# A selective scan's order on three engines, its first chunk's preparation moved among the last projections, and one product moved from GpSimd to ScalarE

## The chip, the cores and the metric
The kernel runs on one core of one Trainium2 chip. Its engines are TensorE (PE in the profile; PEld is its loading of weights), VectorE (DVE), ScalarE (ACT), GpSimd (POOL) and SyncE (SP), which here only issues transfers. The metric is the device time of one execution in microseconds (us), from the runs given below; lower is better.

## The reference, cut to what matters
The input x is (8, 256, 32, 32): 8 batches, 256 channels, N = 1024 tokens. There are 2 heads of 128 channels, 8 states, and a fixed permutation of the tokens for each head.
```
xn  = layernorm(x, over channels)
x_ssm, res, gate = split(silu(in_proj_w (768x256) @ xn + in_proj_b))
xf  = silu(depthwise conv of 3 taps along the tokens (x_ssm))
dbc = dbc_w (34x256) @ xf + dbc_b     # for each head: 1 dt, 8 B, 8 C
dt  = softplus(dbc[:, :, 0])
x_h, dt, B, C = tokens in the order perm[head]
# scan, for each batch and head:
h   = exp(dt_t * A) * h + dt_t * B_t * x_t ;  y_t = C_t . h  + D * x_t
y   = y in the tokens' own order * silu(gate) + res
x   = x + silu(out_proj_w @ y + out_proj_b)
t   = layernorm(x, over channels, by tokens)
x   = t + sum over 8 experts of soft gate[e] * (t @ expert_w[e] + expert_b[e])
```
The last line is added to the tokens before that layernorm. Softmax weights of the gate under 0.1 are dropped and the rest scaled to a sum of 1.

## The kernel before
The whole program is written out by hand for each engine: every engine has a queue of instructions in the written order, and semaphores tie them together. `Signal` wraps a semaphore that is counted up a fixed number of times per batch or chunk. `x_ready.at(q, k)` is the value after k steps of unit q.

**Projections, 0 to about 250 us.** Eight batches, one after the other, some 28.7 us each. PE does in_proj in three products of split fp32 values for six row blocks (`in_proj(b, par, m0, m1)`, m = 0 to 5; m = 0 and 1 are x_ssm, 2 and 3 res, 4 and 5 gate); each m is two groups of six matmuls, L1064. ACT applies silu (`silu_of`, `silu_xf`, `gate_silu`). DVE does layernorm statistics, the convolution (`convolve(b, m)`) and, for each batch, a part of the ranks of the permutation (`ranks`, then `places`, which turns them into addresses). PE's `dbc_by_tokens` (L1074) gives dt, B and C. POOL computes softplus in two parts (`softplus_front`, L592 to L600, and `softplus_back`, L607 to L630) and rstd (`deviations`, L564). POOL also scatters the tokens' numbers to their places in the order, in 16 indirect transfers (`scatter_order(h)`, L644; 8 for head 0 at the end of batch 5, 8 for head 1 at the end of batch 6). SP stores the rows of a batch (x, dt, B, C by tokens: `store_rows`, L442), res (L482) and gate (L490), and loads the order once into `turn` (L463).

**The scan, about 261 to 509 us.** 16 chunks: two groups of four batches, eight chunks of 128 tokens each, which are two blocks of 64 (SUB = 64). A chunk holds ST = 8 tiles, one for each head and batch. For chunk q:

- POOL gathers its rows in the head's order (`gather_rows`, L669, two indirect transfers), three chunks ahead.
- PE `sums_of(q)` (L1102, L1103) sums dt within the blocks. DVE `flatten` (L1631) rearranges B and C, `exponents` (L1638 to `cs`, L1644 to `args`) multiplies the sums by A.
- PE `rows_of` (L1113, L1115) turns B and C to rows. ACT `rows_high` (L850, L854, L856) and DVE `rows_low` (L1662, L1664) split them into high and low parts. ACT `block_decays` (L863). SP `spread` stores these rows (L449) and loads them spread out (L454 into `cr`, named `xhl` or `cr` in the trace, and L456 into `bl`).
- `up_to_token`: dt times a triangle of ones, into `dtri` (L679, POOL). PE `times_of` (L1122, L1124) sums it, DVE `distances` (L1652) subtracts.
- For each state s = 0 to 7: ACT `decays` (L921, exp), PE `products` (L1185, B by C, into three banks in turn), DVE `times_decay` (L1701, their product), POOL `add_state` (L708, sum over states 0 to 6 into `ksum`, `sm` in the trace), then DVE `whole_kernel` (L1713, two instructions: ksum plus state 7 into `kbd`).
- The state carried between blocks: DVE `weigh` (L1677, L1681), PE `states` (L1135) and `columns` (L1142), ACT `columns` (L868 into `cwt`), DVE `next_states` (L1689, L1695), ACT `states_by_tile` (L937, eight scaled copies of 128 columns).
- PE `y_of(q, i)` (L1194: states by C; L1197: x by kbd) for head i, ACT `y_rows` (L927), SP `store_y` (L498). y_of(q-1) runs among the products of chunk q, and so do y_rows(q-1) and whole_kernel(q-1).

The body of chunk q on each engine, before:
```
PE:   rows_of(q+1), products 0-2, times_of(q+1), product 3, y_of(q-1,0), products 4-5,
      y_of(q-1,1), sums_of(q+2), products 6-7, states(q+1), columns(q+1)
ACT:  decays 0-1, rows_high(q+1), block_decays(q+1), decays 2-3, y_rows(q-1,0), decays 4-5,
      y_rows(q-1,1), states_by_tile(q), decays 6-7, columns(q+1)
DVE:  times_decay 0, whole_kernel(q-1), rows_low(q+1), distances(q+1), times_decay 1-3,
      weigh(q+1), times_decay 4-5, flatten(q+2), times_decay 6, exponents(q+2), times_decay 7, next_states(q+1)
POOL: add_state 0-6, up_to_token(q+2), gather_rows(q+3)
SP:   spread(q+1), store_y(q-1)
```
The first chunk is prepared behind the last batch's projections: POOL gathers chunks 0 and 1 once `turn` has landed; PE does sums_of(0) after in_proj m = 4. The last three chunks' places on POOL's queue hold the first gathers of y (`gather_first`, L718).

**The rest, to the end.** For each of 16 half batches: gather y back to the tokens' order, gate, out_proj, layernorm and the experts (L1322), where PE is busy nearly all of the time.

Of the kernel before, what the change touches and what calls it, by code (L numbers as in the profile page):

```python
# [61 lines left out]
def metaformer(nc, x, in_w, in_b, dw_w, dw_b, dbc_w, dbc_b, a_log, d_par, mobius, out_w, out_b,  # L62
# [26 lines left out]
    with ExitStack() as ctx:  # L89
# [126 lines left out]
        ksum = sm[:, 0:4, :].rearrange("p s n -> p (s n)")  # L216
# [3 lines left out]
        names = ysb[1][:, 0:2, :].rearrange("p a n -> p (a n)").bitcast(U32).rearrange("p (j w) -> p j w", w=16)  # L220
# [180 lines left out]
        def _(sync):  # L401
# [142 lines left out]
        def _(pool):  # L544
# [94 lines left out]
            def scatter_order(h):  # L639

                pool.wait_ge(place_ready, 1)
                part_waits(pool)
                for t in range(NT):
# [40 lines left out]
            softplus_front(NB - 2)  # L684
# [6 lines left out]
            up_to_token(Chunk(0))  # L691
            softplus_back(NB - 2)
# [5 lines left out]
            def add_state(c, s):  # L698

                pool.wait_ge(bc_used[s % 3].sem, bc_used[s % 3].at(c.q, s // 3 + 1))  # L700
                if s == 0:
                    pool.wait_ge(dskip_ready, 2)
                    pool.wait_ge(k_ready.sem, k_ready.at(c.q, 0))
                else:
                    pool.wait_ge(summed.sem, summed.at(c.q, s))
                tiles = (v.rearrange("p (t n) -> p t n", n=SUB) for v in (ksum, ee[:, s, :]))
# [17 lines left out]
            def body(q):  # L724
# [3 lines left out]
                if q + 2 < CHUNKS:  # L728
                    up_to_token(Chunk(q + 2))
# [58 lines left out]
        def _(act):  # L788
# [80 lines left out]

            def batch(b):  # L870
# [14 lines left out]
                silu_xf(b, 1)  # L885
                act.wait_ge(gate_stored.sem, gate_stored.at(b, 0))
# [36 lines left out]

            def y_rows(c, h):
# [15 lines left out]
            def body(q):  # L940
# [5 lines left out]
                decays(c, 2, 4)  # L946
                if q:
                    y_rows(Chunk(q - 1), 0)
                else:
                    stage_rows(NB - 1, 0, 1)  # L950
                decays(c, 4, 6)
                if q:
                    y_rows(Chunk(q - 1), 1)
                else:
                    stage_rows(NB - 1, 1, 4)
                states_by_tile(c)
                decays(c, 6, S)
# [51 lines left out]
        def _(pe):  # L1009
# [134 lines left out]
            def batch(b):  # L1144
# [4 lines left out]
                in_proj(b, par, 1, 5)  # L1149
                if ahead:  # L1150
                    normalised_x(b + 1)
# [230 lines left out]
        def _(dve):  # L1382
# [197 lines left out]
            def places():  # L1580

                own.did(dve.tensor_reduce(idxb[:, :, :], racc[:, :, :, :], AX.X, ALU.add))
                own.settle()
                for h in range(HEADS):
                    own.did(dve.tensor_scalar(placef[:, h, :], idxb[:, h, :], float(h * N), None, ALU.add))
                own.settle()
                own.did(dve.tensor_copy(place[:, :, :], placef[:, :, :]))
                own.did(dve.tensor_copy(names, bc(token[:, :, :].rearrange("p t h -> p (t h)"), 2, 16)))
                own.settle()
                dve.sem_inc(place_ready, 1)  # L1590

# [9 lines left out]

            RANKS = {1: (0, 4), 2: (4, 8), 3: (8, 12), 4: (12, 16)}

            def batch(b):
                par, ahead = b % 2, b + 1 < NB
                own1 = Steps(dve, dve1, b + 1)
                if b:
                    dbc_in(b - 1)
                convolve(b, 0)
                if ahead:  # L1610
                    statistics(own1, b + 1)
                convolve(b, 1)
# [8 lines left out]
                if b in RANKS:  # L1621
                    ranks(*RANKS[b])
                if b == 4:
                    places()
# [79 lines left out]
            def whole_kernel(c):  # L1704
# [6 lines left out]
                for i in range(2):  # L1711
                    rr = slice(SUB * i, SUB * i + SUB)
                    dve.tensor_tensor(kbd[rr, :, rr], ksum[rr, :].rearrange("p (s n) -> p s n", s=ST),  # L1713
# [3 lines left out]
            def body(q):  # L1717
                c = Chunk(q)
                times_decay(c, 0)
                if q:  # L1720
                    whole_kernel(Chunk(q - 1))
# [3 lines left out]
                for s in range(1, 4):  # L1725
                    times_decay(c, s)
# [23 lines left out]
            for k in range(2):  # L1750
                dve.wait_ge(mm_full[k].sem, mm_full[k].at(NB - 1, 0))
            dve.memset(cr[0].bitcast(F32), 0.0).then_inc(cr_zero, 1)
            first, second = Chunk(0), Chunk(1)
            flatten(first)
            exponents(first)
# [9 lines left out]
            for i in range(2):  # L1765
                dve.wait_ge(mm_full[i].sem, mm_full[i].at(NB, 0))
            dve.memset(cr[1].bitcast(F32), 0.0).then_inc(cr_zero, 1)
            own.did(dve.memset(batch_no[:, :], 0.0))
            dve.tensor_copy(idxf[:, :, :], idxb[:, :, :]).then_inc(place_ready, 1)
            dve.wait_ge(place_ready, 2)  # L1770
# [215 lines left out]
```

## Time and profile before
| | us |
|---|---|
| median of 3 runs | 1070.61 (1068.48 to 1070.85) |
| the profiled execution, its own time | 1064.97 |
| its span, first to last instruction | 1063.2 |
| PE busy | 930.4 (88%) |
| DVE busy | 771.3 (73%) |
| ACT busy | 508.6 (48%) |
| POOL busy | 505.9 (48%) |
| mean granted clock of TensorE | 0.917 |

Durations come from the one profiled execution, which took a little less than the median of the runs. Busy shares are over the whole span; the stage that the change touches is about a quarter of it. The granted clock is a share of TensorE's full 2.4 GHz; 0.50 is 1.2 GHz. In a timeline a line with xN stands for N instructions in a row, and the bracket gives the engine's idle time before it and what ended it. One name of a tile may be another's: the tiles xin, xtm and xr hold the gathered rows in turn, ysb or ssm or rg what their stage keeps there.

### The profile page before, as it was taken

To read this page: it belongs to the slowest core of one execution; us is meant where nothing else is said; L and a number is where in the kernel's file an instruction comes from. 1 tells how busy PE (TensorE), PEld (TensorE's weight loads), DVE (VectorE), ACT (ScalarE), POOL (GpSimd) and SP (SyncE) were. 2 spreads that over 40 slices of the span, in tenths; PEclk is the share of its full clock that TensorE was granted. 3 is DMA by queue.
4 is the path that set the end of the run, shared out by engine and by line. 5 is a ranking of instruction groups with operands and counts; after the bars stand their busy time and mean duration, and the time that the engine had idled before them with its cause. 6 is when DMAs were issued, how large, how long until landed. Compare 5 with 4: busy or idle time off the path is not lost.

```text
span 1063.2 us, 15454 instructions
## 1 busy us (share of the span) xinstructions
PE 930.4 (88%) x4658; PEld 718.6 (68%) x4658; DVE 771.3 (73%) x2001; ACT 508.6 (48%) x924; POOL 505.9 (48%) x563
## 2 busy tenths in 40 slices
PE   4999999986687678666499999999999999999997
PEld 3887888874454445444367777777777777877776
DVE  5768887534677778775458787787787877878775
ACT  2777877664666665666223333332333323333330
POOL 2066666775887877788650333313333132330000
PEclk8999999996777887778689999999999999999999
DMA  5335674476254343334331131401314013140001
GB/s 162 119 89 171 190 191 147 116 175 177 76 144 126 98 120 109 117 108 156 126 133 44 33 145 39 147 30 39 138 39 158 21 38 138 39 158 20 20 1 39
DMA packets 63687, 110.05 MB, mean 104 GB/s; under 512 B 18538, under 2 KB 44436, under 8 KB 60564
## 3 DMA queue, kind: packets, MB, share of 16 engines
q1 hardware_dynamic: 56468, 91.41, 27.4%
q0 software_dynamic: 7168, 18.03, 5.9%
q8 instruction: 22, 0.36, 0.1%
q14 instruction: 29, 0.24, 0.1%
HBM read 61.51 MB, written 47.92 MB: 103 GB/s over the span
## 4 chain that ended last, share of the span: by engine, by line
PE 69%; DVE 7%; ACT 7%; issue 5%; POOL 5%; DMA 4%; ACTq 0%; SPq 0%; DVEq 0%; another core or an unknown queue 0%; POOLq 0%
PE bank L1322 31%; PE bank L1064 8%; PE bank L1230 4%; PE bank L1255 4%; PE bank L1185 3%; ACT xf L937 3%; PE bank L1283 2%; PE bank L1074 2%; PE bank L1194 2%; POOL sm L708 2%; PE bank L1197 2%; PE bank L1122 2%; PE bank L1092 2%; DMA score_scratch<-score 1%; PE bank L1267 1%
## 5 line engine op out<-in xcount | busy, mean ns | idle before, releaser
L763 POOL TENSOR_TENSOR ssm<-ssm,rg 128x512 f32<-128x512 f32 x30 | 35.2, 1192 | 269.7 <-DVE ssm L1799 269.7
L751 POOL DMA_INDIRECT xtm<-y_scratch,idxu x120 | 119.2, 993 | 68.6 <-issue 34.2
L1322 PE MATMUL bank<-wexph,xhl 128*128 128x512 f32 x512 | 144.9, 405 | 0.1
L1322 PE MATMUL bank<-wexph,cr 128*128 128x512 f32 x512 | 143.4, 401 | 0.1
L708 POOL TENSOR_TENSOR sm<-sm,rg 128x512 f32<-128x512 f32 x96 | 122.4, 1275 | 30.0 <-DVE rg L1701 20.1
L1701 DVE TENSOR_TENSOR rg<-rg,bank 128x512 f32<-128x512 f32 x128 | 83.2, 681 | 60.6 <-ACT rg L921 39.9
L1322 PEld LDWEIGHTS bank<-wexph,xhl 128*128 128x128 f32 x512 | 93.8, 189 | 23.4 <-DVE xf L1903 2.0
L1322 PEld LDWEIGHTS bank<-wexph,cr 128*128 128x128 f32 x512 | 93.4, 189 | 22.0 <-DVE ysb L1903 1.7
L921 ACT ACTIVATE rg<-dists,aown 128x512 f32<-128x512 f32 x128 | 84.7, 714 | 0.0
L1322 PE MATMUL bank<-wexpl,xhl 128*128 128x512 f32 x256 | 80.6, 396 | 0.0
L1322 PE MATMUL bank<-wexpl,cr 128*128 128x512 f32 x256 | 80.3, 395 | 0.0
L1898 DVE SCALAR_TENSOR_TENSOR ysb<-bank,soft,ysb 128x256 f32<-128x256 f32 x128 | 58.3, 479 | 25.1 <-PE bank L1322 23.0
L1898 DVE SCALAR_TENSOR_TENSOR xf<-bank,soft,xf 128x256 f32<-128x256 f32 x128 | 57.8, 479 | 24.4 <-PE bank L1322 21.5
L1064 PE MATMUL bank<-xhl,winh 128*128 128x512 f32 x192 | 55.0, 408 | 4.0 <-ACT ssm L813 2.0
L1064 PE MATMUL bank<-cr,winh 128*128 128x512 f32 x192 | 55.5, 412 | 3.1 <-ACT ssm L813 2.8
L1322 PEld LDWEIGHTS bank<-wexpl,xhl 128*128 128x128 f32 x256 | 48.3, 189 | 11.6
L1322 PEld LDWEIGHTS bank<-wexpl,cr 128*128 128x128 f32 x256 | 48.1, 188 | 11.3
L1903 DVE SCALAR_TENSOR_TENSOR xf<-bank,soft,xf 128x256 f32<-128x256 f32 x128 | 55.5, 475 | 0.0
L1903 DVE SCALAR_TENSOR_TENSOR ysb<-bank,soft,ysb 128x256 f32<-128x256 f32 x128 | 55.5, 475 | 0.0
L813 ACT ACTIVATE rg<-bank,inb 128x512 f32<-128x512 f32 x64 | 43.5, 686 | 14.6 <-PE bank L1064 13.6
L927 ACT ACTIVATE ysb<-bank 128x512 f32<-128x512 f32 x32 | 19.1, 598 | 64.0 <-PE bank L1197 63.6
L592 POOL TENSOR_TENSOR sp<-euler,sp 128x16 f32<-128x16 f32 x8 | 24.4, 3056 | 48.0 <-DVE sp L1563 47.9
(303 smaller groups left out, 2111.9 us busy)
## 6 DMA issues: line engine op xcount, KB each, us to landing
xin<-in_x SPq DMA_DIRECT2D x16, 1024.0 KB, 5.3
res_gate_scratch<-rg SPq DMA_DIRECT2D x16, 1024.0 KB, 10.9
rg<-res_gate_scratch SPq DMA_DIRECT2D x8, 2048.0 KB
y_scratch<-ysb SPq DMA_DIRECT2D x16, 512.0 KB, 3.6
out<-stage SPq DMA_DIRECT2D x16, 512.0 KB, 2.7
rows_scratch<-xr SPq DMA_DIRECT2D x8, 580.0 KB
rows_scratch<-stage SPq DMA_DIRECT2D x8, 580.0 KB
bc_scratch<-r SPq DMA_DIRECT2D x16, 288.0 KB
```

The lines of the kernel that those rows point to most:

```text
L708: pool.tensor_tensor(total, bc(dskip[:, :], 1, ST) if s == 0 else total, new, ALU.add).then_inc(summed.sem, 1)
L751: pool.indirect_dma_start(out=xtm[:, t, h * P:(h + 1) * P], out_offset=None, in_=y_d[b // GB].rearrange("q p s c -> (q p s) c"), in_offset ...
L763: pool.tensor_tensor(z[:, k, :], z[:, k, :], rg[:, k, cols], ALU.add).then_inc(z_ready.sem, 1)
L813: act.activation(dst, bank[2 + hf][:, :], ACT.Silu, bias=inb[:, m:m + 1]).then_inc(mm_used[hf].sem, 1)
L921: act.activation(ee[:, s, :], dist[c.two].rearrange("p t n -> p (t n)"), ACT.Exp, scale=aown[:, s:s + 1]).then_inc(e_ready.sem, 1)
L1064: last = pe.matmul(bank[2 + hf][:, :], w[:, k, m * P:(m + 1) * P], v[:, k, cols], start=(n + k == 0), stop=(n + k == 3))
L1230: last = pe.transpose(dst[:, i * P:(i + 1) * P], src(i), ident[:, :])
L1255: last = pe.matmul(bank[2 + m][:, :], w[:, k, m * P:(m + 1) * P], x_[:, k, :], start=(n + k == 0), stop=(n + k == 3))
L1322: last = pe.matmul(bank[4 + i][:, :], x_[:, k, i * P:(i + 1) * P], w[:, 2 * ep * KC + k:2 * ep * KC + k + KC + 1:KC, :], start=(n + k == 0 ...
L1701: dve.tensor_tensor(ee[:, s, :], ee[:, s, :], bank[BC_BANK + s % 3][:, :], ALU.mult).then_inc(bc_used[s % 3].sem, 1)
L1898: dve.scalar_tensor_tensor(ttm[par][:, i, :], bank[4 + i][:, 0:C], soft[par][:, 2, i, 2 * ep:2 * ep + 1], ttm[par][:, i, :], ALU.mult, ALU ...
L1903: dve.scalar_tensor_tensor(ttm[par][:, i, :], bank[4 + i][:, C:2 * C], soft[par][:, 2, i, 2 * ep + 1:2 * ep + 2], ttm[par][:, i, :], ALU.m ...
```

## The change
Seven things, the first four ahead of the scan:

1. `scatter_order` takes a quarter at a time: head 0 at the ends of batches 3 and 4, the first half of head 1 at the end of batch 5, its second half in batch 6 between deviations(7) and softplus_back(5). `places(h)` is computed at batches 2 and 4 for one head each.
2. On POOL, softplus_front(6) moves behind the gathers of chunks 0 and 1 and up_to_token(0).
3. store_rows(6) moves from SP's queue to ACT's, behind silu_of(7, 5).
4. The first chunk is prepared between the last projections: on PE sums_of(0) after m = 2, rows_of(0) and times_of(0) after m = 3, and dbc_by_tokens(7) after m = 4. On DVE the zeroing of cr[0] moves to the start of batch 7, and flatten(0) and exponents(0) between its two convolutions. On ACT rows_high(0) and block_decays(0) move ahead of silu_of(7, 4).
5. `ksum` is doubled, so add_state(q, 0) waits for whole_kernel(q-2) rather than whole_kernel(q-1).
6. up_to_token(q+2) is ACT's: eight ACTIVATE Copy of 64 columns with dt as the scale by partition.
7. The chunk's order, by the diff's bodies: ACT issues decays 2 to 7, states_by_tile(q), both y_rows(q-1), up_to_token(q+2), columns(q+1). PE issues products 0 and 1, rows_of(q+1), product 2, times_of(q+1), product 3, the rest as before. On DVE whole_kernel(q-1) moves behind times_decay 1, and exponents(q+2) ahead of times_decay 6.

The diff, cut to its core:
```diff
-        ksum = sm[:, 0:4, :].rearrange("p s n -> p (s n)")
+        ksum = [sm[:, 4 * i:4 * i + 4, :].rearrange("p s n -> p (s n)") for i in range(2)]
...
-                    store_rows(b - 1)
                     sync.wait_ge(cr_zero, 1)
...
-                for t in range(NT):
+            def scatter_order(h, part):
+                for t in range(part * TPH, (part + 1) * TPH):
...
                 deviations(b + 1)
+                if b == NB - 2:
+                    scatter_order(1, 1)
                 if b:
                     softplus_back(b - 1)
...
-                if b == NB - 3:
-                    scatter_order(0)
-                if b == NB - 2:
-                    scatter_order(1)
+                if NB - 5 <= b < NB - 2:
+                    scatter_order(*divmod(b - NB + 5, 2))
...
-            softplus_front(NB - 2)
             pool.wait_ge(order_loaded, 16 * HEADS)
...
             up_to_token(Chunk(0))
+            softplus_front(NB - 2)
             softplus_back(NB - 2)
...
-                    pool.wait_ge(k_ready.sem, k_ready.at(c.q, 0))
+                    if c.q:
+                        pool.wait_ge(k_ready.sem, k_ready.at(c.q - 1, 0))
...
-                if q + 2 < CHUNKS:
-                    up_to_token(Chunk(q + 2))
                 if q == 0:
                     softplus_back(NB - 1)
...
+                if not ahead:
+                    act.wait_ge(consts_ready, 1)
+                    rows_high(Chunk(0))
+                    block_decays(Chunk(0))
                 act.wait_ge(gate_stored.sem, gate_stored.at(b, 0))
                 silu_of(b, 4)
...
+                silu_of(b, 5)
                 if not ahead:
-                    act.wait_ge(consts_ready, 1)
-                    rows_high(Chunk(0))
-                    block_decays(Chunk(0))
-                silu_of(b, 5)
+                    store_rows(b - 1)
...
+            def up_to_token(c):
+
+                act.wait_ge(xr_ready[c.row].sem, xr_ready[c.row].at(c.turn4, 32))
+                act.wait_ge(b_full.sem, b_full.at(c.q, 0))
+                for t in range(ST):
+                    last = act.activation(dtri[:, t, :], tri[:, :], ACT.Copy, scale=dt_of(c)[:, t:t + 1])
+                last.then_inc(dtri_ready.sem, 1)
...
-                decays(c, 2, 4)
                 if q:
-                    y_rows(Chunk(q - 1), 0)
+                    decays(c, 2, S)
+                    states_by_tile(c)
+                    for h in range(HEADS):
+                        y_rows(Chunk(q - 1), h)
...
+                if q + 2 < CHUNKS:
+                    up_to_token(Chunk(q + 2))
                 if q + 1 < CHUNKS:
                     columns(Chunk(q + 1))
...
+                    in_proj(b, par, 1, 3)
                     pe.wait_ge(consts_ready, 1)
                     pe.wait_ge(rows_staged.sem, rows_staged.at(b - 1, 4))
                     sums_of(Chunk(0))
-                    dbc_by_tokens(b)
+                    in_proj(b, par, 3, 4)
                     rows_of(Chunk(0))
                     times_of(Chunk(0))
+                    in_proj(b, par, 4, 5)
+                    dbc_by_tokens(b)
                     in_proj(b, par, 5, MI)
...
+                products(c, 0, 2)
                 if q + 1 < CHUNKS:
                     rows_of(Chunk(q + 1))
-                products(c, 0, 3)
+                products(c, 2, 3)
...
+                if not ahead:
+                    zero_rows(0, NB - 1)
                 convolve(b, 0)
                 if ahead:
                     statistics(own1, b + 1)
+                else:
+                    flatten(Chunk(0))
+                    exponents(Chunk(0))
                 convolve(b, 1)
...
                 times_decay(c, 0)
-                if q:
-                    whole_kernel(Chunk(q - 1))
                 if q + 1 < CHUNKS:
                     rows_low(Chunk(q + 1))
                     distances(Chunk(q + 1))
-                for s in range(1, 4):
-                    times_decay(c, s)
+                times_decay(c, 1)
+                if q:
+                    whole_kernel(Chunk(q - 1))
+                times_decay(c, 2)
+                times_decay(c, 3)
...
                 if q + 2 < CHUNKS:
                     flatten(Chunk(q + 2))
+                    exponents(Chunk(q + 2))
                 times_decay(c, 6)
-                if q + 2 < CHUNKS:
-                    exponents(Chunk(q + 2))
                 times_decay(c, 7)
```

## Rows read from the trace of the kernel before
**Rows 1.** Windows: us; busy us (count) PE, PEld, DVE, ACT, POOL; PEclk, DMA share, GB/s.
```profile
325.10:355.80 30.70, 22.48 (x114) 14.95 (x113) 23.84 (x48) 19.52 (x51) 24.04 (x21) 0.78 0.38 112
...
426.30:429.40 3.10, 0.00 (x0) 0.00 (x0) 1.01 (x4) 2.82 (x8) 2.62 (x3) 1.00 0.36 93
...
430.20:437.00 6.80, 6.23 (x14) 3.82 (x14) 6.14 (x14) 3.83 (x11) 4.89 (x6) 0.50 0.45 128
...
214.00:226.00 12.00, 9.24 (x62) 8.01 (x62) 0.78 (x5) 5.78 (x9) 9.85 (x9) 0.97 1.08 269
```

**Rows 2.** Chain of waits, 428 to 448 us: start, us, what.
```profile
441.07 2.43 ACT xf L937 x8
```

**Rows 3.** Timeline, chunk 430 to 444 us: start, us, engine, line, operation, idle before.
```profile
430.69 1.32 ACT L921 ACTIVATE rg<-dists,aown 128x512 f32<-128x512 f32 x2
...
432.85 0.28 ACT L856 ACTIVATE r<-bank 64x128 fp32r<-64x128 f32 x1
...
433.21 1.44 DVE L1713 TENSOR_TENSOR kbd<-sm,rg 64x512 f32<-64x512 f32 x2
...
434.69 0.48 DVE L1662 TENSOR_TENSOR r<-bank,r 64x64 fp32r<-64x64 f32 x3
...
436.13 1.87 DVE L1701 TENSOR_TENSOR rg<-rg,bank 128x512 f32<-128x512 f32 x3
...
436.89 6.95 POOL L708 TENSOR_TENSOR sm<-sm,rg 128x512 f32<-128x512 f32 x5 [0.79 <-DVE rg L1701]
...
438.57 1.02 PE L1194 MATMUL bank<-xf,cwt 128*128 128x512 f32 x2
...
439.43 1.05 PE L1197 MATMUL bank<-xr,kbd 128*128 128x128 f32 x8
...
440.58 0.60 ACT L927 ACTIVATE ysb<-bank 128x512 f32<-128x512 f32 x1 [0.40 <-PE bank L1197]
```

**Rows 4.** Timeline at the scan's end, POOL and DVE.
```profile
512.45 2.76 POOL L773 TENSOR_TENSOR ssm<-ssm,stage 128x512 f32<-128x512 f32 x2 [3.74 <-DVE ssm L1943]
513.01 2.75 DVE L1713 TENSOR_TENSOR kbd<-sm,rg 64x512 f32<-64x512 f32 x2
```

**Rows 5.** Timeline of PE, chunks 14 and 15.
```profile
478.55 1.63 PE L1185 MATMUL bank<-xhl,bl 128*128 128x512 f32 x3
...
491.59 2.44 PE L1185 MATMUL bank<-cr,bl 128*128 128x512 f32 x4 [3.01 <-DMA bl<-bc_scratch]
...
494.60 2.04 PE L1194 MATMUL bank<-xf,cwt 128*128 128x512 f32 x2 [0.57 <-issue]
...
496.43 1.91 PE L1197 MATMUL bank<-xr,kbd 128*128 128x128 f32 x8
```

**Rows 6.** Timelines of POOL and SP's queue, ahead of the scan.
```profile
212.87 2.15 SPq L442 DMA_DIRECT2D rows_scratch<-stage  x2
...
222.14 0.96 POOL L644 DMA_INDIRECT order_scratch<-ysb,place  x1 [0.30 <-issue]
...
227.71 1.42 SPq L463 DMA_DIRECT2D turn<-order_scratch  x2
...
232.00 1.62 POOL L669 DMA_INDIRECT xin<-rows_scratch,turn  x1 [1.97 <-DMA turn<-order_scratch]
...
246.01 1.08 SPq L449 DMA_DIRECT2D bc_scratch<-r  x1
...
254.19 2.73 SPq L454 DMA_DIRECT2D xhl<-bc_scratch  x8
...
262.45 1.26 POOL L708 TENSOR_TENSOR sm<-dskip,rg 128x512 f32<-128x512 f32 x1 [4.70 <-DVE rg L1701]
```

**Rows 7.** Timeline of PE, last batch to first chunk.
```profile
231.94 1.21 PE L1064 MATMUL bank<-cr,winh 128*128 128x512 f32 x4
...
238.24 0.36 PE L1102 MATMUL bank<-xin,cumu 128*128 128x8 f32 x2 [0.46 <-issue]
...
260.74 1.65 PE L1185 MATMUL bank<-xhl,bl 128*128 128x512 f32 x3 [9.56 <-DMA bl<-bc_scratch]
```

More of the change, by code:

```diff
@@ L219, in metaformer @@
               for i in (1, 2) for j in range(8)]
-        names = ysb[1][:, 0:2, :].rearrange("p a n -> p (a n)").bitcast(U32).rearrange("p (j w) -> p j w", w=16)
+        names = ysb[0][:, 0:2, :].rearrange("p a n -> p (a n)").bitcast(U32).rearrange("p (j w) -> p j w", w=16)
         z = ssm[:, :, 0:HALF]
@@ L637, in low_experts @@
                                    ALU.subtract).then_inc(wexp_low, 1)
[L639 to L641 removed]
+            def scatter_order(h, part):
+                pool.wait_ge(place_ready, h + 1)
                 part_waits(pool)
[L643 removed]
+                for t in range(part * TPH, (part + 1) * TPH):
                     pool.indirect_dma_start(
@@ L702, in add_state @@
                     pool.wait_ge(dskip_ready, 2)
-                    pool.wait_ge(k_ready.sem, k_ready.at(c.q, 0))
+                    if c.q:
+                        pool.wait_ge(k_ready.sem, k_ready.at(c.q - 1, 0))
                 else:
                     pool.wait_ge(summed.sem, summed.at(c.q, s))
-                tiles = (v.rearrange("p (t n) -> p t n", n=SUB) for v in (ksum, ee[:, s, :]))
+                tiles = (v.rearrange("p (t n) -> p t n", n=SUB) for v in (ksum[c.two], ee[:, s, :]))
                 total, new = tiles
@@ L868, in columns, with store_rows @@
                 act.activation(cwt[c.four][:, :], bank[A_BANK][:, 0:P], ACT.Copy).then_inc(a_free.sem, 1)
+            def store_rows(b):
+                act.wait_ge(rows_ready.sem, rows_ready.at(b, 4))
+                act.wait_ge(rows_staged.sem, rows_staged.at(b, 4))
+                for hf, v in enumerate(staged[b % 2]):
+                    act.dma_start(rows_d[b // GB][:, hf * TPH * HEADS:(hf + 1) * TPH * HEADS, b % GB, :],
+                                  v.rearrange("p t (h c) -> p (t h) c", h=HEADS)).then_inc(rows_stored[b % 2].sem, 16)
             def batch(b):
@@ L945, in body @@
                     block_decays(Chunk(q + 1))
-                decays(c, 2, 4)
                 if q:
-                    y_rows(Chunk(q - 1), 0)
+                    decays(c, 2, S)
+                    states_by_tile(c)
+                    for h in range(HEADS):
+                        y_rows(Chunk(q - 1), h)
                 else:
+                    decays(c, 2, 4)
                     stage_rows(NB - 1, 0, 1)
-                decays(c, 4, 6)
-                if q:
-                    y_rows(Chunk(q - 1), 1)
-                else:
+                    decays(c, 4, S)
                     stage_rows(NB - 1, 1, 4)
-                states_by_tile(c)
-                decays(c, 6, S)
+                    states_by_tile(c)
+                if q + 2 < CHUNKS:
+                    up_to_token(Chunk(q + 2))
                 if q + 1 < CHUNKS:
@@ L1148, in batch @@
                     x_by_tokens(b + 1)
-                in_proj(b, par, 1, 5)
                 if ahead:
+                    in_proj(b, par, 1, 5)
                     normalised_x(b + 1)
@@ L1578, in ranks, with places, rows_by_rank @@
                     own.settle()
-            def places():
-                own.did(dve.tensor_reduce(idxb[:, :, :], racc[:, :, :, :], AX.X, ALU.add))
+            def places(h):
+                own.did(dve.tensor_reduce(idxb[:, h, :], racc[:, h, :, :], AX.X, ALU.add))
                 own.settle()
-                for h in range(HEADS):
-                    own.did(dve.tensor_scalar(placef[:, h, :], idxb[:, h, :], float(h * N), None, ALU.add))
+                own.did(dve.tensor_scalar(placef[:, h, :], idxb[:, h, :], float(h * N), None, ALU.add))
                 own.settle()
-                own.did(dve.tensor_copy(place[:, :, :], placef[:, :, :]))
-                own.did(dve.tensor_copy(names, bc(token[:, :, :].rearrange("p t h -> p (t h)"), 2, 16)))
+                own.did(dve.tensor_copy(place[:, h, :], placef[:, h, :]))
+                if h == 0:
+                    own.did(dve.tensor_copy(names, bc(token[:, :, :].rearrange("p t h -> p (t h)"), 2, 16)))
                 own.settle()
                 dve.sem_inc(place_ready, 1)
+            def rows_by_rank():
                 own.did(dve.tensor_copy(idxu[:, :, :], idxb[:, :, :]))
@@ L1600, in places, with zero_rows @@
                 ts(idxb[:, 1, :], idxb[:, 1, :], float(SUB * ST), None, ALU.add)
+            def zero_rows(i, b):
+                for hf in range(2):
+                    dve.wait_ge(mm_full[hf].sem, mm_full[hf].at(b, 0))
+                dve.memset(cr[i].bitcast(F32), 0.0).then_inc(cr_zero, 1)
             RANKS = {1: (0, 4), 2: (4, 8), 3: (8, 12), 4: (12, 16)}
@@ L1622, in batch @@
                     ranks(*RANKS[b])
+                if b in (2, 4):
+                    places(b // 2 - 1)
                 if b == 4:
-                    places()
+                    rows_by_rank()
             def flatten(c):
@@ L1712, in whole_kernel @@
                     rr = slice(SUB * i, SUB * i + SUB)
-                    dve.tensor_tensor(kbd[rr, :, rr], ksum[rr, :].rearrange("p (s n) -> p s n", s=ST),
+                    dve.tensor_tensor(kbd[rr, :, rr], ksum[c.two][rr, :].rearrange("p (s n) -> p s n", s=ST),
                                       ee[rr, S - 1, :].rearrange("p (s n) -> p s n", s=ST),
@@ L1749, in _ @@
                 batch(b)
-            for k in range(2):
-                dve.wait_ge(mm_full[k].sem, mm_full[k].at(NB - 1, 0))
-            dve.memset(cr[0].bitcast(F32), 0.0).then_inc(cr_zero, 1)
             first, second = Chunk(0), Chunk(1)
-            flatten(first)
-            exponents(first)
             rows_low(first)
@@ L1764, in _ @@
             next_states(first)
-            for i in range(2):
-                dve.wait_ge(mm_full[i].sem, mm_full[i].at(NB, 0))
-            dve.memset(cr[1].bitcast(F32), 0.0).then_inc(cr_zero, 1)
+            zero_rows(1, NB)
             own.did(dve.memset(batch_no[:, :], 0.0))
             dve.tensor_copy(idxf[:, :, :], idxb[:, :, :]).then_inc(place_ready, 1)
-            dve.wait_ge(place_ready, 2)
+            dve.wait_ge(place_ready, 3)
             dve.tensor_copy(idxu[:, :, :], idxf[:, :, :]).then_inc(idx3_ready.sem, 1)
```

1 line of the change is left out of this document (removed).

## The prediction
> **What bounds the kernel now.** I read the page first, then windows, then the chain. The page's busy shares name PE, but the change touches only the scan and its preparation, so what counts is what ends last there. Two scan chunks take 30.70 us, 15.35 each, in which PE is busy 22.48, DVE 23.84, POOL 24.04 and ACT 19.52 [rows 1]: no engine is full, so the chunk is a ring of waits. The chain of waits runs on PE through products, times_of and both y_of, then on ACT through the copy of y and states_by_tile (2.43 us [rows 2]), which hold back decay 6 and with it exponents and states. Second, PE's clock: it idles 3.10 us before states, and the 6.80 us that begin 0.8 us later are granted 0.50, 1.2 GHz, not 2.4 [rows 1]. Those slow microseconds now fall on rows_of, products 0 to 3, times_of and the head of the first y_of. The reader is to see that the low clock is paid by whatever follows PE's idle time. Third, the front: chunk 0's first product waits for a row of steps that begins with the load of the order and the first gather; that is worked out below.
>
> **The steady chunk, part by part.** Below, "first y_of" is y_of(q-1, 0).
>
> *Order.* ACT now issues decays 2 to 7 and states_by_tile ahead of both y copies, so decay 6 no longer waits behind y_of and the 2.43 us of states_by_tile; that stall goes. What is late next is y_of itself: whole_kernel, which PE's y_of waits for, moves from behind times_decay 0 to behind rows_low, distances and times_decay 1. PE has nothing between product 3 and y_of. Behind the waiting y_of are products 4 and 5, and behind those times_decay 4 and 5 on DVE, add_state on POOL, and exponents(q+2).
>
> *dt times the triangle.* POOL's one instruction becomes eight ACT copies with a pointer scale, 64 columns each. The nearest row has eight of 128 columns in 2.43 us [rows 2]. Bounds: 1.2 us, by the halved columns alone, and 2.43. I take 1.9, as a copy of the same form is unlikely to lose more than a quarter with half its columns. It stands on ACT between the last y copy and columns(q+1), whose copy is what rows_of(q+2) and the next pair of decays wait for.
>
> *The ring of the new order, at full clock.* Two decays, then rows_high, from 430.69 to the end of its last copy 433.13: 2.4 [rows 3]. rows_low and distances, 434.69 to the start of the next at 436.13: 1.4. times_decay 1, one of three in 1.87 us: 0.6. whole_kernel 1.4. First y_of, from 438.57 to 439.43 + 1.05: 1.9 [rows 3]. Products 4 and 5: 0.5 (three take 1.63 at half clock [rows 5]). Second y_of 1.9. ACT's y copy 0.6 [rows 3], dtri copies 1.9, columns copy 0.3 (as the one at 432.85 [rows 3]), waits between engines some 0.3. Sum 13.3; of the first term about 0.5 is ACT's wait for PE and the previous state, and about 0.2 laps over: 12.6.
>
> *The port of DVE and POOL.* In the scan whole_kernel now takes 1.44 for two, as POOL only issues gathers then. Where POOL ran two adds beside it, it took 2.75 [rows 4]. Both changes bring adds there: whole_kernel comes later, and add_state(q, 0) needs only k_ready of chunk q-2, as ksum is doubled. Bounds 0 and 1.3; I take 1.1, since POOL's adds are close together (five in 6.95 [rows 3]) and can start right after times_decay 0. Ring: 13.7. The Trainium skill ("SBUF — State Buffer", Who interferes with whom) says that a DVE instruction with two SBUF inputs and a GpSimd one exclude each other on a shared port pair for their whole length; it speaks against this move, and the trace agrees [rows 4]. By that rule the ring is 13.7, and without it 12.6.
>
> *The clock.* PE's idle time now lies between product 3 and y_of: distances' tail, times_decay 1 and whole_kernel, 0.7 + 0.6 + 1.4 + 1.1, which is 3.8, or 2.7 without the port wait. That is about as long as the 3.10 us that a half-clock stretch follows today, and y_of would then be what stands in it: at half clock it took 3.7 us in chunk 15 (494.60 to 496.43 + 1.91), against 1.9 [rows 3, 5]. If the low stretch covers the first y_of and products (+1.8, +0.5) and half of what is left (+1.1) it costs 3.4; if it falls on times_of and the products, which lie beside DVE's work, 0. I take 2.0. Ring: 15.7 against 15.35, +0.35 a chunk; over the 12 intervals from chunk 2 to 14: **+4.2**.
>
> **The front.** Scatter quarters (0,0) to (1,0) move to batches 3 to 5, where POOL waits for DVE's statistics anyway; without that cover each is 5.1 us. Quarter (1,1) now stands before softplus_back(5): four of 1.26 [rows 6] delay it by 5.1 us, so SP's store_rows(5), at 212.87 now [rows 6], goes at 217.9, and behind it on SP the res and gate stores and then the turn load L463. The load's own wait ends earlier (its last scatter, at 222.14 now, is done by 212), but it is issued at about 222, right behind stores that now take the 12 us from 214 to 226 at a share of 1.08 (269 GB/s, 3.2 MB [rows 1]) and that start some 5 us later. It lands at 231 to 233, and the first gather, at 232.00 now [rows 6], comes no earlier. softplus_front(6), behind up_to_token(0) now, took nothing off this path.
> PE now reaches sums_of(0) after m=2, at 231.9, where m=3 stood [rows 7]; sums_of waits until about 239 (238.24 now). m=3 and m=4, 5.8 us together (231.94 to 238.24 less the gap of 0.46), come after it. rows_of stands behind m=3, which may find the clock fallen: 2.9 us, or 5.8 at half. So rows_of starts at 242 to 245 and, with some 3 us of ACT's copies and rows_low (an estimate), the rows leave for bc_scratch at about 248. They are no longer behind store_rows(6), so I put their landing at 3 to 4 us, not the 8.2 from the issue at 246.01 to L454 at 254.19 [rows 6]; from L454 to the product is 6.55 [rows 6, 7]. First product: 258 to 260, against 260.74. The memset before convolve(7,0) lies beside PE's wait; without that cover it delays the last convolution by its length.
> store_rows(6), on ACT behind silu_of(7,5) and so behind in_proj m=5, leaves when m=5 is done, some 258; gather(2), for which it is waited, precedes POOL's first add: 266 to 268 (262.45 now [rows 6]). The seven adds then run unbroken (five in 6.95 [rows 3]: 9.8) and no dtri follows, so POOL catches up. Chunk 2 begins 1 us earlier: **-1** (bounds -3 and +3).
>
> **The tail.** From chunk 14 to 15 it is 13.04 now [rows 5]; there the new ring has no dtri copies: 13.8, **+0.7**.
>
> Sum: -1 + 4.2 + 0.7 = +3.9 on the profiled execution's 1064.97 us, 1068.9. The runs' median, 1070.61, is 1.0053 times that execution: 1074.5.
>
> **Rivals.** 0.2% (2.1 us) is about what a measurement of this kernel can tell from no change.
> A, the other side: *the clock stays up through y_of*. For it: y_of is longer than states was, and the idle time may come out under 3.1 us; if the port wait is absent too, it is 1.1 shorter. Against: the row of 3.10. The period is 13.7, or 14.2 with a remainder of low clock: 12 x (-1.65 or -1.15), with front and tail, is -20 or -14, a run of 1050 or 1056; without the port wait too it would be less still. It decides from a period under 15.2. Chance 0.22.
> B, faster too: *the turn load is not held by the stores*, and lands at 227: sums_of comes 5 us earlier, PE hardly waits, and chunk 2 starts 7 us earlier. -7 + 4.2 + 0.7 = -2.1 to -4: 1067.5. The full DMA engines of those 12 us [rows 1] speak against it. Chance 0.15.
> C: *the change does nothing that shows*: DVE's 23.84 us a pair plus the port wait make the period 15.3, whatever the order; front and tail cancel. 1068.5 to 1072.7. Chance 0.21.
> Forecast, +2.2 to +12: 0.42; its own range 1073 to 1083.
> Faster 0.37, same 0.21, slower 0.42. Range: up to 1083, where the low clock costs 2.7 a chunk; down to 1055, which leaves out the fuller part of A.
>
> **What would show it.** Two chunks against 30.70. L1713: 1.44 for two now [rows 3], 2.5 if the port is shared. L1194 and L1197: their half-clock lengths on the first y_of, and where PE's idle window stands. The eight copies: 1.9 us together. Dates of the first gather, sums_of(0), first product, first add. If y_of runs at its 1.9 in most chunks, A is true and my sign is wrong; if L463 lands by 228, B.

## The result and the profile after

The changed kernel takes 1076.12 us (median of 20 runs, 1069.23 to 1083.51), the kernel before 1067.20 (20 runs, 1063.58 to 1070.85) in the same sessions. The ratio is 1.0079, with a 95% interval of 1.006 to 1.0097: 8.4 us slower (the medians alone would give 8.9). The forecast was slower by 0.36%. The profiled execution of the changed kernel is also its fastest, 1069.23 us, 4.3 us over that of the kernel before, so the traces show only about half of the difference.

The windows of the two chunks from 356.10 to 386.80, to be held against [rows 1]; the columns are us, busy us (count) of PE, PEld, DVE, ACT and POOL, then PEclk, DMA share and GB/s:

```profile
356.10:386.80 30.70, 20.93 (x113) 13.82 (x112) 28.43 (x48) 23.16 (x67) 22.16 (x19) 0.89 0.38 113
```

DVE is busy for 28.43 of 30.70 us, where it was 23.84. Nothing was added to its work. PE's mean clock even rose, from 0.78 to 0.89. DVE, nearly full, is now the engine that bounds a chunk.

From the first times_decay of chunk 2 to that of chunk 14 the changed kernel needs 187.90 us, 15.66 a chunk; before it was 184.23, 15.35. The two rows in the timeline of DVE, then the same two of the kernel before:

```profile
292.92 0.69 DVE L1737 TENSOR_TENSOR rg<-rg,bank 128x512 f32<-128x512 f32 x1
...
480.82 0.69 DVE L1737 TENSOR_TENSOR rg<-rg,bank 128x512 f32<-128x512 f32 x1
```

```profile
295.21 0.69 DVE L1701 TENSOR_TENSOR rg<-rg,bank 128x512 f32<-128x512 f32 x1 [1.68 <-PE bank L1185]
...
479.44 0.69 DVE L1701 TENSOR_TENSOR rg<-rg,bank 128x512 f32<-128x512 f32 x1 [0.90 <-PE bank L1185]
```

The mean hides a difference. In this fastest execution chunks 4 to 9 take 15.35 us each on average, exactly as before. Of the 3.67 us that the twelve chunks lose, 2.2 lie in chunks 2 and 3 and 1.1 in chunks 11 to 13.

One chunk of the changed kernel in its timeline (start, us, engine, line, operation, idle before), to be held against [rows 3]. L1749 is whole_kernel, L708 the add, L1214 and L1217 are y_of, L1713 is weigh, L1667 flatten, L937 the eight copies of dt times the triangle:

```profile
404.87 0.67 DVE L1737 TENSOR_TENSOR rg<-rg,bank 128x512 f32<-128x512 f32 x1
404.98 1.28 POOL L708 TENSOR_TENSOR sm<-dskip,rg 128x512 f32<-128x512 f32 x1
405.46 3.03 DVE L1749 TENSOR_TENSOR kbd<-sm,rg 64x512 f32<-64x512 f32 x2
406.40 1.54 POOL L708 TENSOR_TENSOR sm<-sm,rg 128x512 f32<-128x512 f32 x1
...
408.59 1.10 PE L1214 MATMUL bank<-xf,cwt 128*128 128x512 f32 x2 [4.19 <-issue]
...
409.53 1.75 PE L1217 MATMUL bank<-xin,kbd 128*128 128x128 f32 x8
409.73 0.92 DVE L1713 TENSOR_TENSOR bwx<-xr,argx 64x64 f32<-64x64 f32 x1
...
413.44 0.98 DVE L1667 COPY bct<-xr 128x128 f32<-128x128 f32 x1
...
415.02 2.00 ACT L937 ACTIVATE dtri<-tri,xr 128x64 f32<-128x64 f32 x8
```

whole_kernel's pair takes 3.03 us, where it took 1.44 [rows 3], and two adds of POOL lie beside it. PE stands still for 4.19 us before the first y_of, which starts when whole_kernel is done. The eight copies take 2.00 us.

Groups of DVE's instructions from 340 to 440 us (busy, mean ns of one, idle before), the changed kernel:

```profile
L1749 DVE TENSOR_TENSOR kbd<-sm,rg 64x512 f32<-64x512 f32 x14 | 20.2, 1446 | 0.2
L1713 DVE TENSOR_TENSOR bwx<-xr,argx 64x64 f32<-64x64 f32 x8 | 8.7, 1083 | 0.1
L1680 DVE TENSOR_TENSOR args<-cs,acol 128x256 f32<-128x256 f32 x6 | 5.8, 968 | 0.2
L1667 DVE COPY bct<-xr 128x128 f32<-128x128 f32 x3 | 2.9, 976 | 0.0
```

The same stretch of before:

```profile
L1713 DVE TENSOR_TENSOR kbd<-sm,rg 64x512 f32<-64x512 f32 x14 | 9.7, 690 | 0.2
L1644 DVE TENSOR_TENSOR args<-cs,acol 128x256 f32<-128x256 f32 x6 | 9.1, 1509 | 0.2
L1677 DVE TENSOR_TENSOR bwx<-xr,argx 64x64 f32<-64x64 f32 x8 | 6.3, 787 | 0.1
```

There the means are 690 ns for whole_kernel, 787 for weigh, 1509 for args, and flatten took 280. A chunk has two of the first two and one of the others: 1.51 + 0.59 - 0.54 + 0.70 = 2.3 us more, which is the difference of the windows, (28.43 - 23.84) / 2.

The front, from the timelines of SP, POOL, PE and DVE, to be held against [rows 6, 7]. L668 is gather_rows, L1119 sums_of, L1205 products, L1629 the zeroing of cr[1], which was not moved, and L1737 times_decay:

```profile
216.50 5.97 SPq L463 DMA_DIRECT2D turn<-order_scratch  x2
...
227.93 1.08 POOL L668 DMA_INDIRECT xin<-rows_scratch,turn  x1 [15.25 <-DMA turn<-order_scratch]
...
233.42 0.56 PE L1119 MATMUL bank<-xin,cumu 128*128 128x8 f32 x2 [10.31 <-DMA xin<-rows_scratch,turn]
...
253.23 3.47 DVE L1629 MEMSET cr<- 128x4096 f32 x1 [0.80 <-issue]
253.29 0.73 PE L1205 MATMUL bank<-xhl,bl 128*128 128x512 f32 x2 [1.50 <-DMA bl<-bc_scratch]
...
257.18 0.69 DVE L1737 TENSOR_TENSOR rg<-rg,bank 128x512 f32<-128x512 f32 x1
...
262.55 1.10 POOL L668 DMA_INDIRECT xr<-rows_scratch,turn  x1 [7.51 <-DMA rows_scratch<-xr]
...
264.94 1.27 POOL L708 TENSOR_TENSOR sm<-dskip,rg 128x512 f32<-128x512 f32 x1
...
281.42 1.06 POOL L668 DMA_INDIRECT xr<-rows_scratch,turn  x1 [0.28 <-issue]
...
288.03 1.34 DVE L1667 COPY bct<-xr 128x128 f32<-128x128 f32 x1 [6.20 <-DMA xr<-rows_scratch,turn]
```

This execution was 3.3 us ahead long before: rstd of batch 4 starts at 118.51 (121.80 before). All times that follow are measured from that start, in both kernels. The first gather is 0.8 us earlier and the first product 4.2. PE waits 10.31 us for the gather.

The 4.2 us are not kept. The zeroing of cr[1] takes DVE 3.47 us; before, it lay in the wait for the first product, and now it ends behind it, so the first times_decay is only 1.2 us earlier. On POOL, gather(2) waits 7.51 us for the late rows of batch 6, and the first add comes 5.8 us later. POOL catches up a part: gather(3), behind the seven adds and softplus_back(7), is 2.4 us later, and DVE's flatten(3) waits 6.20 us for its rows, where it waited 4.20. The first times_decay of chunk 2 is 1.0 us later.

### The profile page after: what moved, and what is told of

The parts are those of the page before. It is cut to its first block, busy times and chain, and to the rows that moved or that the text cites. A ratio compares the mean times of both kernels' runs of the same rounds, so it can differ in the third digit from the quotient of the medians.

```text
span 1067.5 us, 15556 instructions
## 1 busy us (share of the span) xinstructions
PE 920.8 (86%) x4658; PEld 709.8 (66%) x4658; DVE 801.6 (75%) x2003; ACT 534.7 (50%) x1036; POOL 489.7 (46%) x549
## 4 chain that ended last, share of the span: by engine, by line
PE 66%; issue 10%; POOL 8%; DVE 7%; DMA 5%; ACT 3%; SPq 0%; another core or an unknown queue 0%; ACTq 0%; DVEq 0%; POOLq 0%
PE bank L1343 32%; PE bank L1081 5%; PE bank L1251 4%; PE bank L1276 4%; PE bank L1205 4%; PE bank L1214 3%; PE bank L1217 3%; PE bank L1304 2%; POOL sm L708 2%; PE bank L1091 2%; DMA score_scratch<-score 1%; PE bank L1139 1%; PE bank L1288 1%; DMA rows_scratch<-xr 1%; POOL rstd L563 1%
## 5 line engine op out<-in xcount | busy, mean ns | idle before, releaser
L708 POOL TENSOR_TENSOR sm<-sm,rg 128x512 f32<-128x512 f32 x96 | 126.0, 1312 | 52.9 <-DVE rg L1737 43.8
L1214 PE MATMUL bank<-xf,cwt 128*128 128x512 f32 x64 | 48.3, 847 | 60.6 <-issue 60.6
L1737 DVE TENSOR_TENSOR rg<-rg,bank 128x512 f32<-128x512 f32 x128 | 83.1, 681 | 13.0 <-PE bank L1205 8.9
L1214 PEld LDWEIGHTS bank<-xf,cwt 128*128 128x128 f32 x64 | 15.1, 264 | 69.4 <-issue 67.2
```

The lines of the kernel that those rows point to most:

```text
L708: pool.tensor_tensor(total, bc(dskip[:, :], 1, ST) if s == 0 else total, new, ALU.add).then_inc(summed.sem, 1)
L1214: pe.matmul(dst[:, :], cwt[c.four][:, :], hx[c.two][:, GB * i:GB * (i + 1), :].rearrange("p t c -> p (t c)"), start=True, stop=False, skip ...
L1737: dve.tensor_tensor(ee[:, s, :], ee[:, s, :], bank[BC_BANK + s % 3][:, :], ALU.mult).then_inc(bc_used[s % 3].sem, 1)
```

## The experiments

Twelve kernels, each with five rounds against the kernel before on the same chip. The period is that from chunk 2's first times_decay to chunk 14's, a twelfth of it, in the one profiled execution.

| kernel | median us | ratio to before | 95% interval | period us |
|---|---|---|---|---|
| the changed one | 1076.12 | 1.0079 | 1.006 to 1.0097 | 15.66 |
| scan_only | 1068.82 | 1.0045 | 1.0024 to 1.0067 | 15.99 |
| front_only | 1067.55 | 1.0051 | 1.0032 to 1.0071 | 15.44 |
| scatter_only | 1065.65 | 1.0004 | 0.9989 to 1.002 | 15.43 |
| front_123 | 1068.78 | 1.0031 | 1.0012 to 1.005 | 15.60 |
| wk_back | 1044.99 | 0.9842 | 0.9823 to 0.9861 | 13.89 |
| adds_wait | 1047.45 | 0.9824 | 0.9797 to 0.9851 | 14.11 |
| fill10 | 1071.57 | 1.0082 | 1.0063 to 1.0101 | 15.86 |
| adds_fill | 1043.45 | 0.9717 | 0.9691 to 0.9744 | 12.99 |
| scan_wk | 1043.00 | 0.9782 | 0.976 to 0.9804 | 13.71 |
| scatter_wk | 1050.74 | 0.9794 | 0.9751 to 0.9836 | 14.05 |
| wk_rows_sp | 1058.98 | 0.9858 | 0.9832 to 0.9883 | 13.97 |
| wk_dtri_pool | 1061.46 | 0.9894 | 0.9869 to 0.9918 | 14.49 |

The medians of the twelve are from sessions in which the kernel before took 1062.16, 1065.14 and 1072.77 us, so kernels of different sessions are compared by their ratios. A ratio differs a little from the quotient of the medians. The kernels without parts 5 to 7 have `ksum` doubled too, but add_state waits in them as before.

**scan_only and front_only: which half loses.** The change was cut in two: parts 5 to 7 on the front of before, and parts 1 to 4 with the chunk of before.

> Parts 5 to 7 of the change alone (doubled ksum, dtri on ACT, the chunk's order); the front is as before. Theory 1, the scan's new order costs the time (half clock on the first y_of, whole_kernel beside the adds): 5 to 12 us slower than before, two chunks 31.2 or more against 30.70. Theory 2, the front costs it: within 2 us of before, two chunks 30.7.

> Parts 1 to 4 of the change alone (scatters in quarters, first chunk prepared among the last projections); the chunk's order, dtri on POOL and the wait of add_state are as before. Theory 1: 1 to 6 us faster than before, as the first product comes at about 253 and not 261, of which the late rows of batch 6 take some back; two chunks 30.7. Theory 2: 5 us or more slower than before.

Both lose, 0.45% and 0.51%. The scan's loss, 4.8 us, is just under the 5 to 12 of theory 1, and two of its chunks take 32.0 on average, over the 31.2 there. The front's is not as theory 1 has it, which had the front faster. Together they are somewhat more than the whole, 0.79%.

**wk_back: one move undone.**

```diff
                 times_decay(c, 0)
+                if q:
+                    whole_kernel(Chunk(q - 1))
                 if q + 1 < CHUNKS:
                     rows_low(Chunk(q + 1))
                     distances(Chunk(q + 1))
                 times_decay(c, 1)
-                if q:
-                    whole_kernel(Chunk(q - 1))
```

> The changed kernel with one move undone: whole_kernel(q-1) stands right behind times_decay 0 again. Theory 1: it leaves the adds' company (0.7 each, not 1.65) and PE's idle time ahead of y_of shrinks to about 1 us, so the first y_of runs at full clock: two chunks 28 to 30, 8 to 20 us faster than the changed kernel. Rival, the ring is set by ACT (dtri copies, y copies), wherever whole_kernel stands: two chunks 31, no change.

It is 1.6% faster than before and 2.4% (25 us) faster than the changed kernel, which is more than either expectation allowed. A window of two of its shorter chunks (the mean of two is 27.8):

```profile
380.40:407.10 26.70, 23.07 (x113) 15.23 (x113) 24.00 (x48) 22.92 (x66) 20.75 (x18) 0.76 0.44 128
```

DVE's 24.00 is near the 23.84 of before. All of the rest of parts 5 to 7 is in this kernel, so that rest is worth 1.5 us a chunk (15.35 to 13.89). Moving whole_kernel took it away. Whether that is by its late place or by the adds that then lie beside it, this run does not tell; the next one does.

**adds_wait: late, but with no add beside it.** The move stays; only the wait of part 5 is undone.

```diff
                 if s == 0:
                     pool.wait_ge(dskip_ready, 2)
-                    if c.q:
-                        pool.wait_ge(k_ready.sem, k_ready.at(c.q - 1, 0))
+                    pool.wait_ge(k_ready.sem, k_ready.at(c.q, 0))
```

> The changed kernel, whole_kernel(q-1) still behind times_decay 1, but add_state(q, 0) waits for it again, so no add runs beside it. If the wait for the port there is the cost: the two of L1713 take 1.4 (2.3 to 3.0 now) and two chunks take 28.5 to 30, 8 to 15 us faster than the changed kernel. If the cost is that whole_kernel stands late in DVE's queue, wherever the adds are: two chunks 30.5 to 31.5, within 4 us of the changed kernel.

A line that makes POOL wait longer makes the kernel 2.5% faster than the changed one, again more than expected. From its timeline:

```profile
401.98 1.40 DVE L1748 TENSOR_TENSOR kbd<-sm,rg 64x512 f32<-64x512 f32 x2
403.48 1.84 PE L1213 MATMUL bank<-xf,cwt 128*128 128x512 f32 x2 [2.83 <-issue]
403.55 1.27 POOL L707 TENSOR_TENSOR sm<-dskip,rg 128x512 f32<-128x512 f32 x1 [1.74 <-DVE kbd L1748]
...
405.11 1.91 PE L1216 MATMUL bank<-xin,kbd 128*128 128x128 f32 x8
```

whole_kernel is back at 1.40 and the add comes behind it. The reader is also to see that the first y_of, 3.54 us from 403.48 on, is at half clock, and yet this chunk takes 13.9 us. Over the twelve chunks DVE is busy 11.75 us a chunk, where it was 14.10 in the changed kernel. So the cost was the overlap of whole_kernel with POOL's adds, the port wait of the prediction, and not where whole_kernel stands: late without adds (0.9824) it is as fast as early (0.9842).

**fill10 and adds_fill: the clock.** Ten matmuls whose product is not used keep PE busy until whole_kernel is done; fill10 is the changed kernel with them, adds_fill is adds_wait with them.

```diff
+                pe.wait_ge(y2_used[i].sem, y2_used[i].at(c.q, 0))
+                dst = bank[SY_BANK + i]
+                if i == 0 and 0 < c.q < CHUNKS - 1:
+                    for _ in range(10):
+                        pe.matmul(dst[:, :], bl[1 - c.two][:, 0, :], cr[1 - c.two][:, 0, :], start=True, stop=True)
                 pe.wait_ge(hx_ready.sem, hx_ready.at(c.q, 1))
                 pe.wait_ge(k_ready.sem, k_ready.at(c.q, 2))
-                pe.wait_ge(y2_used[i].sem, y2_used[i].at(c.q, 0))
-                dst = bank[SY_BANK + i]
```

> The changed kernel with ten more matmuls of 512 columns in each of 14 chunks, on PE ahead of the first y_of, into the bank that y_of then overwrites; their product is not used. If the low clock is what costs: the stretch at half clock goes, y_of's L1214 takes 0.59 and not 1.19, two chunks 28 to 29.5, 10 to 20 us faster than the changed kernel. If the port and DVE's queue cost it: 31.0 to 31.3 as now, or more.

> adds_wait with the ten extra matmuls of fill10 ahead of the first y_of. adds_wait takes 13.9 a chunk with the first y_of at half clock (1.19 and 1.06 for its L1194 pair). If that half clock costs next to nothing, because DVE's queue fills the ring meanwhile: 13.6 to 14.2 a chunk, within 5 us of adds_wait. If it costs the 2.0 that the prediction gave it: 12 to 12.5 a chunk, 15 us or more faster.

In fill10 the first y_of runs at full clock in 14 of 16 chunks (4 in the changed kernel), and nothing is won: 1.0082. Two of its chunks have DVE busy 28.12 of 31.90 us. But the low clock did not go, a part of it moved: over the twelve chunks the mean clock rose only from 0.85 to 0.90, and 19 of 36 matmuls of times_of ran at half clock, where it was 3. In adds_fill, where DVE has no port wait at whole_kernel, the same matmuls gain 1.1% (11 us), and the mean clock is 0.96. One chunk of each, adds_wait first:

```profile
412.70:426.60 13.90, 10.45 (x59) 6.90 (x57) 11.54 (x25) 11.54 (x35) 10.51 (x10) 0.88 0.40 125
```

and adds_fill, with its timeline:

```profile
388.80:401.10 12.30, 11.25 (x69) 7.75 (x68) 11.47 (x24) 11.43 (x34) 10.91 (x10) 1.00 0.48 141
```

```profile
402.71 2.49 PE L1213 MATMUL bank<-xhl,bl 128*128 128x512 f32 x10
...
404.05 1.40 DVE L1751 TENSOR_TENSOR kbd<-sm,rg 64x512 f32<-64x512 f32 x2
...
405.60 1.10 PE L1216 MATMUL bank<-xf,cwt 128*128 128x512 f32 x2 [0.39 <-DVE kbd L1751]
```

13.9 and 12.3 us: in these chunks the half clock cost 1.6 us. Over the twelve the means are 14.11 and 12.99, so it cost 1.1 on average. Both of my expectations for adds_fill were thus too simple; it lies between them, by its median and by its mean period, and only its best chunks reach the second.

**scan_wk and scatter_wk: without the lossy half of the front.**

> The front of before, and the scan's parts 5 to 7 with whole_kernel(q-1) right behind times_decay 0. If the gain of undoing that one move and the loss of the front add up: two chunks 27 to 28, 19 to 24 us faster than before (1 to 6 faster than wk_back against the same reference). If the front's loss came only together with the old chunk order: as wk_back, 17 faster.

> The parts that did not lose, together: scatters in quarters, the scan's parts 5 to 7 with whole_kernel(q-1) right behind times_decay 0; first chunk and rows of batch 6 as before. Expected at scan_wk or up to 3 us under it: 20 to 26 us faster than before. If the quarters only shift the clock's phase: as scan_wk.

scan_wk has wk_back's chunk on the front of before: 0.9782 against 0.9842. Without the changed front 0.6% is won with the other chunk order too, so the losses add up. The quarters of part 1 bring nothing (0.9794).

**scatter_only, front_123 and wk_rows_sp: where the front loses.** scatter_only is before with part 1; front_123 with parts 1 to 3; wk_rows_sp is wk_back with store_rows(6) on SP again.

> Before with part 1 alone (scatters and places in quarters). If the scatters ahead of softplus_back(5) are what costs in the front: 3 to 6 us slower than before. If it is the late rows of batch 6 or PE's wait among the projections: within 2 us of before, or up to 3 faster as POOL's ten microseconds in batch 6 fall away.

> Before with parts 1 to 3 (scatters, softplus_front(6) later, rows of batch 6 stored by ACT behind silu_of(7, 5)); the first chunk is prepared behind in_proj m = 4 as before. If the late rows cost: 3 to 6 us slower than before, first add of chunk 0 at 264 or later. If PE's wait for the gather among the last projections costs (part 4, left out here): within 2 us of before.

> wk_back with the rows of batch 6 stored by SP ahead of the first spread, as before, and all else of the front as changed. If the late rows, and with them gather(2) and gather(3), are the front's loss: gather(2) some 5 us earlier than in wk_back, 2 to 5 us faster than it, near scan_wk. If it is part 4: no change to wk_back.

Part 1 costs nothing: 1.0004. With parts 2 and 3 it is 1.0031. The first spread's loads (L454), gather(2) and the first add of scatter_only (first fence) and of front_123 (second, with the rows' store by ACT and the first product):

```profile
251.57 2.82 SPq L454 DMA_DIRECT2D xhl<-bc_scratch  x8
...
257.05 1.11 POOL L669 DMA_INDIRECT xr<-rows_scratch,turn  x1 [0.52 <-issue]
...
259.44 1.27 POOL L708 TENSOR_TENSOR sm<-dskip,rg 128x512 f32<-128x512 f32 x1
```

```profile
253.18 1.03 ACTq L874 DMA_DIRECT2D rows_scratch<-xr  x2
253.96 5.41 SPq L454 DMA_DIRECT2D xhl<-bc_scratch  x8
...
263.19 1.10 POOL L668 DMA_INDIRECT xr<-rows_scratch,turn  x1 [2.64 <-DMA rows_scratch<-xr]
...
264.13 1.65 PE L1194 MATMUL bank<-xhl,bl 128*128 128x512 f32 x3 [7.84 <-DMA bl<-bc_scratch]
...
265.84 1.26 POOL L707 TENSOR_TENSOR sm<-dskip,rg 128x512 f32<-128x512 f32 x1 [0.30 <-DVE rg L1720]
```

gather(2) now ends a wait for the rows; in scatter_only it did not. But that wait is not what the first add waits for in front_123: its bracket names DVE, which waits for the first product, and PE waits 7.84 us for the spread. gather(2) was done 0.3 us before. The rows' store was issued 0.8 us ahead of the spread's loads, which then took 5.41 us to issue and not 2.82, and the first product is 4.0 us later than in scatter_only (from rstd of batch 4). So in front_123 the rows' store most likely delays the spread; that it is the cause was not tested by itself. In the changed kernel, where part 4 has the spread loaded before the store, gather(2) is the late one. wk_rows_sp, which stores the rows on SP again beside part 4, gained nothing (0.9858 against 0.9842). In its SP queue the rows stand ahead of the first spread, and that one is late:

```profile
251.15 1.01 SPq L442 DMA_DIRECT2D rows_scratch<-xr  x2
252.34 1.26 SPq L449 DMA_DIRECT2D bc_scratch<-r  x1
261.97 2.73 SPq L454 DMA_DIRECT2D xhl<-bc_scratch  x8
```

The spread's rows take 9.6 us from their issue to the first load behind them (8.2 in [rows 6]), and PE waits 13.89 us for the first product. With part 4 either the rows or the spread is late. Which of parts 2, 3 and 4 costs how much of the 0.5% stays open: their steps are 0.27% (parts 2 and 3) and 0.20% (part 4), with intervals that overlap.

**wk_dtri_pool: the eight copies.** scan_wk with up_to_token(q+2) on POOL again, behind the adds, as in the kernel before.

> scan_wk with dt times the triangle on POOL again. If ACT's eight copies (2.0 us) stand in the ring: two chunks 25 to 26.5, faster than scan_wk. If POOL's 1.24 us delays the gathers and the next adds more than that: two chunks 27 to 29, up to 15 us slower than scan_wk.

0.9894 against 0.9782: moving the product to ACT is worth 1.1%, some 12 us, though it takes ACT 2.00 us where it takes POOL 1.06 here and took it up to 1.24 before. The second expectation held: two chunks take 29.0 us.

## Why the prediction was right, and where it was not

**The ring.** The forecast period of 15.7 was measured at 15.66, and the three terms of it can be taken apart by the mean periods. Without low clock and without the port wait at whole_kernel I had 12.6 (the terms as rounded add up to 13.2 before the 0.7 is taken off, not 13.3): adds_fill shows 12.99, with a little low clock left. The low clock I had at 2.0: 1.1 by adds_wait against adds_fill. The port wait I had at 1.1: 1.5 by the changed kernel against adds_wait (15.66 to 14.11). The bound of 1.3 came from two adds beside the pair [rows 4]; one chunk measured 3.03, 1.6 more than 1.44 [rows 3], and weigh and flatten wait longer too, which I had left out. So one term was 0.9 too high and two together 0.8 too low: that their sum came out is luck. It is luck also in that the middle chunks of the trace take 15.35, as before. That the new order of the scan costs time does not rest on it: scan_only lost 0.45%, and its chunks 4 to 9 take 15.94 each.

**What the sum had wrong is its form.** I put the port wait and the low clock one after the other on the same ring. The runs show that they do not add up that way: the same ten matmuls are worth 1.1 us a chunk once the port wait is gone and nothing beside it (15.66 to 15.86). That the low clock is free while DVE is full would fit this, but is not shown, as fill10 also moved low clock to times_of.

**Rival A** (the clock stays up through y_of, and the kernel is faster) is refuted: with the first y_of at full clock the changed kernel is as slow. **Rival C** (DVE's work plus the port wait make the period, nothing shows) had half of the mechanism: DVE was busy 28.43 of 30.70 us, and the middle chunks take 15.35. Its outcome is refuted, as the loss of 0.79% is clear of noise, and so is its "whatever the order": wk_back takes 13.89. **Rival B** gave a date, the turn load by 228. The load landed at 226.7 and 227.1, and the first gather came at 227.93. But measured from rstd of batch 4 that gather is 0.8 us earlier, not 5, so the gain that B named did not exist. By the same measure the scatters of quarter (1,1) delayed store_rows(5) by 3.1 us (212.71 against 212.87 [rows 6]), not 5.1: it stands 4.5 us further behind deviations(7), which itself came 1.3 earlier. The load was issued at 216.50 and was held, as forecast, by the stores: 9.8 us to its landing, where it was 2.7.

**The front** is the step that failed: "Chunk 2 begins 1 us earlier". Alone, parts 1 to 4 cost 0.51%, 5.4 us, outside the bounds of -3 and +3. PE's wait was 10.3 us where I had 7. gather(2) waits for the rows of batch 6, as I had said, and the first add came 5.8 us later, where I had 4 to 6. What failed is "so POOL catches up": behind the seven adds softplus_back(7) and gather(3) still stand, and gather(3) was 2.4 us late. The zeroing of cr[1], which the sum left out, took back 3 of the 4.2 us of the first product. The traces show less than the medians: to the start of chunk 2, from rstd of batch 4, the changed front costs 2.5 us in front_only against before, 3.4 in the changed kernel against scan_only, and 0.3 in wk_back against scan_wk. Where the rest of the 5.4 lies stays open.

**The tail** was +0.7, measured +1.5 (14.55 against 13.05 between the first times_decay of chunks 14 and 15).

The scan alone was thus forecast at +4.9 and measured at 0.45%, 4.8 us; the front at -1 and +5.4. The sign was right for the first half, and the size fell short by the second.

## What to carry to other kernels

Before moving a VectorE instruction with two SBUF inputs, or giving it a second buffer so that GpSimd need not wait, look at what GpSimd runs beside it: a wait that keeps the two apart can be worth more than the overlap. Two costs on one ring need not add up; take one away at a time, and then both. An earlier first product is worth nothing if another transfer that the stage also needs becomes late, or if work that lay hidden in the old wait comes to stand behind it.

## What the runs showed of the hardware

- A pair of VectorE adds of 64x512, 1.40 us alone, took 3.03 with GpSimd adds beside it, more than the 2.75 of [rows 4]; a copy of 128x128, 0.28 alone, took 0.98, and a product of 64x64, 0.21 to 0.32, took 0.92 to 1.26 (one of its two took 1.25 in the kernel before already). times_decay, one of whose inputs lies in PSUM, kept its 0.68 beside the same adds. The Trainium skill ("SBUF — State Buffer", Who interferes with whom) says that copies in a two-port mode and instructions with two SBUF inputs contend with GpSimd for the shared pair; the durations of this trace agree, though it does not show in which mode the copy ran.
- ScalarE's copy with a pointer scale took 334 ns for 64 columns in the changed kernel and 389 for 128 in the kernel before (eight in 2.00 and 2.43 us).
- Unneeded matmuls in PE's idle time raised the granted clock of a chunk to 1.00 and made the kernel 1.1% faster (adds_fill against adds_wait), but only once the port wait at whole_kernel was gone. adds_fill, at 0.9717, is by its ratio the fastest of all kernels here: 29 us less than the kernel before on its chip.
